# Second layer of a fused transformer: the attention product and the transposed key scores move from between two substitutions into the second one, and each inverse is fetched three quarters through the substitution before it

## Chip, cores and metric

One core of one Trainium2 chip. The time is the device time of one execution in microseconds (us); each figure for a kernel is the median of several runs.

## What is computed

Four batches of 256 tokens with 256 channels pass through two layers. Each layer gates the input with a bidirectional recurrence, adds an attention block, gates again and adds a feed-forward block (ternary weights in layer 0; eight experts, two per token, in layer 1). The change touches only layer 1's attention, cut here to what matters (16 heads of 16, per batch):

```python
s = einsum('bihd,bjhd->bhij', k, k) * scale          # rotated keys with themselves
p = softmax over j < i of s                           # strictly lower triangle
A = eye(T) + p * beta                                 # unit lower triangular, 256 x 256 per head
u = solve_triangular(A, v, lower=True)                # forward substitution
attn = softmax over j <= i of (q k^T * scale)
o = einsum('bhij,bjhd->bihd', attn, u) @ Wo
```

## The kernel before, in words

Every engine runs its own in-order stream. All streams are generated from one list of steps, `ORDER`, written by `make_order`; VectorE alone follows `DVE_ORDER`, which `lag` derives from it by holding a side step back until the next half of the chain has been issued. A step is a tuple (kind, ..., batch, index), and each engine does its own part of it at that place of its list: for `("solve", b, s, half)` TensorE multiplies, VectorE copies the result out of PSUM, and SyncE (SP) issues four small DMAs that move the solution to where the attention product reads it.

The triangular solve of a batch is a chain of eight block rows. `solve b s` multiplies the inverse of a 32x32 diagonal block with the right side (PE line 886, copied by VectorE line 1842); `update b s` multiplies the result with the blocks below (PE line 1117), and VectorE turns it (line 1828) and forms the next right side (line 1831). Each of the two steps is done in two halves of eight heads. The chain needs, per batch:

- `kscores` in five groups (k with k, strictly causal): TensorE, then VectorE maxima (lines 1660 to 1669), then ScalarE exponentials with row sums (line 1385). `kmax` turns the maxima (PE line 1013, ScalarE copy line 1344, four DMAs), `kdiag` recomputes the diagonal blocks transposed (TensorE, ScalarE line 1363), `den` and `blocks` prepare them on VectorE (lines 1800 to 1811), and GpSimd (POOL) inverts them (from line 2052 to 2061). `inverse` is VectorE's transposition of that inverse into place (line 1820); POOL's next `blocks` waits for it, since it works in one buffer.
- `kprobs` in four groups: the transposed k by k scores (TensorE, ScalarE line 1370). They are the factors that `update` reads.

Beside it runs the causal attention: `scores` in eight groups (TensorE; maxima on VectorE, lines 1679 and 1680), `minus` and `max` (VectorE lines 1687 to 1693, PE line 1013, ScalarE line 1344, one DMA), `probs` in eight groups (TensorE, ScalarE lines 1354 and 1355), `pv` (attention times solution: 64 matmuls of TensorE, ScalarE copy line 1397), `otr`, `oT`, `wo` (PE lines 1060, 1070, 886) and the next `gate`.

`pv b` waits until all DMAs of the solution of batch b have landed (semaphore `u_moved`), and VectorE waits for the same before it copies the first link of batch b + 1, because that overwrites their source. `kscores`, `kprobs`, `kdiag`, `scores`, `probs`, `pv`, `otr`, `oT` and `wo` share a ring of two PSUM slots ("mid"): each waits on TensorE until the slot of the step two before it was given back by the engine that reads it.

The lists `ahead[b]` in `make_order` hold the side work of batch b; `spread` deals it out evenly behind the 15 units of the chain (`solve 0`, then `update` and `solve` in turn). Before, the loop put `inverse b` in front of `solve b 0`, and behind the chain of batch b three groups of `kprobs b + 2`, `pv b`, and the fourth group.

## Time and profile before

| | us |
|---|---|
| median of 3 runs (793.16 to 796.17) | 794.1 |
| the profiled execution's own time | 791.78 |
| its span, first to last instruction | 789.9 |
| PE busy / DVE busy / ACT busy / POOL busy | 515.3 / 555.2 / 326.1 / 213.7 |
| mean granted TensorE clock (share of full speed) | 0.776 |
| layer 1's four substitutions, in the trace | about 428.9 to 628.6 |

The page gives busy time by engine, the span in 40 slices, the DMA queues, the chain that ended last and the costliest groups. Behind it stand views of the trace: tables by stretch, the timeline of an engine (start, duration, engine, line, operation, and in brackets the idle time before it with the engine or queue that ended it), the chain in order of time, and groups by line. A timeline row can hold several instructions that follow each other closely (x32); its duration runs from the first start to the last end, and can reach into the next step.

### The profile page before, as it was taken

How to read it: one execution, taken by the hardware profiler on the slowest of the kernel's cores; microseconds unless marked ns; L12 is line 12 of the kernel's file. 1: busy time of each engine (PE TensorE's matmuls, PEld its weight loads, DVE VectorE, ACT ScalarE, POOL GpSimd, SP SyncE). 2: the span in 40 equal slices, each digit the busy share in tenths (PEclk: the TensorE clock that was granted, in tenths of full speed). 3: DMA queues.
4: the chain of work that ended last, by engine and by line, in shares of the span. 5: the costliest groups of instructions: out<-in, count | busy, mean ns of one | idle time of the engine just before them, and what ended most of it. 6: DMA issues, size and time to landing. Idle time of an engine off the chain costs nothing. (4 is left out here: it accounts for less than half of the span.)

```text
span 789.9 us, 18230 instructions
## 1 busy us (share of the span) xinstructions
PE 515.3 (65%) x7549; PEld 424.6 (54%) x7549; DVE 555.2 (70%) x1116; ACT 326.1 (41%) x755; POOL 213.7 (27%) x313
## 2 busy tenths in 40 slices
PE   0362655885696770446557467677877874799995
PEld 0251544774575560334445355456665653699995
DVE  6999699797859966685673677456466536668861
ACT  4344343543456422016444600451321334367771
POOL 2000000000000000100884870881683001335443
PEclk9876856896698985675567575768798956699999
DMA  8145023050000010463016033002102148257622
GB/s 312 38 95 121 1 62 59 1 116 6 1 2 1 21 34 0 101 151 74 4 40 127 5 78 57 6 7 49 61 10 62 13 160 280 80 148 200 202 27 27
DMA packets 48211, 56.07 MB, mean 71 GB/s; under 512 B 25136, under 2 KB 42048, under 8 KB 43648
## 3 DMA queue, kind: packets, MB, share of 16 engines
q1 hardware_dynamic: 44784, 49.90, 24.3%
q0 software_dynamic: 3344, 4.99, 3.3%
q8 instruction: 60, 0.98, 0.5%
q14 instruction: 23, 0.19, 0.1%
HBM read 43.15 MB, written 10.49 MB: 68 GB/s over the span
## 5 line engine op out<-in xcount | busy, mean ns | idle before, releaser
L886 PE MATMUL psum<-arena 32*32 32x16 f32 (+22 forms) x5713 | 357.0, 272 | 213.5 <-DVE arena L1608 76.2
L886 PEld LDWEIGHTS psum<-arena 128*32 128x32 f32 (+8 forms) x5713 | 283.5, 127 | 285.9 <-DVE arena L1608 79.8
L2061 POOL TENSOR_TENSOR arena<-arena 128x31 f32<-128x31 f32 (+15 forms) x124 | 68.3, 551 | 9.7
L2059 POOL TENSOR_TENSOR arena<-arena 128x31 f32<-128x31 f32 (+15 forms) x124 | 64.6, 521 | 9.7
L1385 ACT ACTIVATE psum<-psum,arena 128x256 f32<-128x256 f32 (+7 forms) x128 | 45.7, 363 | 30.4 <-DVE arena L1669 30.1
L1679 DVE TENSOR_REDUCE arena<-psum 128x2 f32<-128x512 f32 (+1 forms) x48 | 41.3, 861 | 13.4 <-PE psum L886 12.8
L1578 DVE TENSOR_TENSOR_SCAN arena<-arena 128x255 f32<-128x255 f32 x64 | 42.5, 726 | 11.4 <-ACT arena L1297 11.3
L1354 ACT ACTIVATE arena<-psum 128x512 f32<-128x512 f32 (+1 forms) x48 | 35.4, 737 | 36.1 <-PE psum L886 36.0
L2040 POOL DMA_DIRECT2D arena<-wq x1 | 0.9, 862 | 171.8 <-PE psum L886 171.8
L1297 ACT ACTIVATE arena<-arena 128x255 f32<-128x255 f32 x64 | 27.2, 498 | 46.4 <-DVE arena L1564 46.4
L2085 POOL DMA_INDIRECT out<-arena x16 | 31.2, 1947 | 48.6 <-DVE arena L1985 46.5
L2075 POOL DMA_INDIRECT arena<-dispatched,arena x16 | 19.7, 1229 | 87.0 <-DVE arena L1952 83.3
L1967 DVE TENSOR_TENSOR fc_second_parts<-arena,fc_first_parts 128x2048 fp32r<-128x2048 f32 x16 | 36.6, 2289 | 7.8 <-ACT fc_first_parts L1489 7.7
L886 PE MATMUL psum<-input_first_parts,fc_first_parts 128*128 128x256 f32 x128 | 38.9, 304 | 1.3 <-DVE input_second_parts L1961 1.3
L1564 DVE TENSOR_TENSOR_SCAN arena<-arena 128x256 f32<-128x256 f32 x64 | 39.0, 671 | 0.5
L1461 ACT ACTIVATE psum<-psum,arena 128x256 f32<-128x256 f32 x64 | 24.6, 448 | 35.5 <-PE psum L886 35.5
L1117 PE MATMUL psum<-arena 32*32 32x224 f32 (+6 forms) x896 | 37.3, 311 | 1.7 <-issue 1.5
L886 PE MATMUL psum<-fc_first_parts,hidden_first_parts 128*128 128x256 f32 x128 | 36.8, 288 | 2.5 <-DVE hidden_second_parts L1978 2.5
L886 PE MATMUL psum<-input_second_parts,fc_first_parts 128*128 128x256 f32 x128 | 38.0, 297 | 0.0
L886 PE MATMUL psum<-input_first_parts,fc_second_parts 128*128 128x256 f32 x128 | 37.9, 296 | 0.0
L1828 DVE STREAM_TRANSPOSE arena<-psum 128x64 f32<-128x64 f32 x56 | 13.8, 246 | 33.8 <-PE psum L1117 33.0
L886 PE MATMUL psum<-fc_second_parts,hidden_first_parts 128*128 128x256 f32 x128 | 36.2, 283 | 0.0
(186 smaller groups left out, 936.3 us busy)
## 6 DMA issues: line engine op xcount, KB each, us to landing
arena<-fc SPq DMA_DIRECT2D x16, 1024.0 KB, 5.0
arena<-parts SPq DMA_DIRECT2D x40, 256.0 KB, 4.6
parts<-arena SPq DMA_DIRECT2D x16, 384.0 KB, 3.5
arena<-parts SPq DMA_DIRECT2D x40, 128.0 KB, 5.2
arena<-arena SPq DMA_DIRECT2D x128, 8.0 KB, 1.8
arena<-xT SPq DMA_DIRECT2D x1, 1024.0 KB, 10.1
arena<-w1T SPq DMA_DIRECT2D x1, 1024.0 KB, 10.1
arena<-w2T SPq DMA_DIRECT2D x1, 1024.0 KB, 12.1
```

The source lines that it names most:

```text
L886: return nc.tensor.matmul(out, lhsT, rhs, start=start, stop=stop)
L1117: last = nc.tensor.matmul(acc(half)[rows, qq, (s + 1) * BLK:T], ublk[rows, s, q, :], later[b % 2][s][rows, q, :], start=s == 0 and qq == 0 ...
L1297: A(scan[s + 1][:, ct, 0:T - 1], scan[s][:, ct, 0:T - 1], ACT.Copy, scale=back[:, i:i + 1]).then_inc(scaled, 1)
L1354: step_(A(prob[:, hs, 0:T], hi, ACT.Exp, scale=scale))
L1385: ins = A(s_, s_, ACT.Exp, bias=nbias[:, n:n + 1], accum_out=ncc[b][:, n:n + 1])
L1564: ins = V.tensor_tensor_scan(scan[s][:, ct, :], dd, src[:, ct, bt(b)], 0.0, ALU.mult, ALU.add)
L1578: st(V.tensor_tensor_scan(scan[s][:, ct, T - 2::-1], dd, scan[s + 1][:, ct, T - 2::-1], scan[s][:, ct, T - 1:T], ALU.mult, ALU.add))
L1679: st(V.tensor_reduce(mneg[:, H + j * n:H + (j + 1) * n], hi, axis=AX.X, op=ALU.max, negate=True))
L1967: V.tensor_tensor(second[:], fcw[e % NW][i], first[:].bitcast(F32), ALU.subtract).then_inc(w_second[i], 1)
L2059: link(G_.tensor_tensor(tmp, A3[:, k + 1:BLK, k:k + 1].to_broadcast([P, rows, w]), X3[:, k:k + 1, 0:w].to_broadcast([P, rows, w]), ALU.mult))
L2061: ins = G_.tensor_tensor(X3[:, k + 1:BLK, 0:w], X3[:, k + 1:BLK, 0:w], tmp, ALU.add)
L2085: G_.indirect_dma_start(out=d["out"], out_offset=bass.IndirectOffsetOnAxis(ap=ids[:, 2 * e + s:2 * e + s + 1], axis=0), in_=eo[e % 2][:, s ...
```

## The change

For b = 0, 1, 2 it places the side work anew. `pv b`, the first entry of the old list of batch b + 1, and all four groups of `kprobs b + 2` (where there is such a batch) become the first entries of `ahead[b + 1]`, so that they are dealt out behind the links of the substitution of batch b + 1. `inverse b + 1` becomes an entry of `ahead[b]` at three quarters of its length. `inverse 0` stands in front of the loop, and `solve 0` of a batch stands alone as first unit. Behind the last batch `route`, `count` and `pv 3` are where they were. `lag` recognises the start of a substitution by `solve` in place of `inverse`. No instruction is added or removed.

```diff
     for b in range(B):
-
-        solve = [[("inverse", b), ("solve", b, 0, 0), ("solve", b, 0, 1)]]
+        if b + 1 < B:
+            ahead[b + 1] = [[("pv", 1, b)]] + ahead[b + 1][:1] + ([[step] for step in groups("kprobs", 1, b + 2)] if b + 2 < B else []) \
+                + ahead[b + 1][1:]
+            ahead[b].insert(len(ahead[b]) * 3 // 4, [("inverse", b + 1)])
+    o += [("inverse", 0)]
+    for b in range(B):
+
+        solve = [[("solve", b, 0, 0), ("solve", b, 0, 1)]]
         for s in range(1, NS):
             solve += [[(kind, b, s - (kind == "update"), half) for half in range(2)] for kind in ("update", "solve")]
         o += sum(spread(solve, ahead[b]), [])
-        if b + 2 < B:
-            o += groups("kprobs", 1, b + 2)[:3]
-        else:
-            o += [("route", i) for i in range(B - 1) if b == B - 1] + [("count",)] * (b == B - 1)
-        o += [("pv", 1, b)]
-        if b + 2 < B:
-            o += groups("kprobs", 1, b + 2)[3:]
+    o += [("route", i) for i in range(B - 1)] + [("count",), ("pv", 1, B - 1)]
...
-        if step[0] == "inverse":
+        if step[0] == "solve":
             solving = True
```

Three places show what moves. The first is ScalarE behind batch 0's substitution: line 1344 is the copy of `max`, 1370 `kprobs 2`, 1397 `pv 0`, 1385 `kscores 3`. Before, and then now:

```order
L1344 ACTIVATE arena<-psum 64x128
L1370 ACTIVATE arena<-psum 128x896
L1370 ACTIVATE arena<-psum 128x768
L1370 ACTIVATE arena<-psum 128x128
L1370 ACTIVATE arena<-psum 128x640
L1370 ACTIVATE arena<-psum 128x256
L1397 ACTIVATE arena<-psum 128x1024
L1370 ACTIVATE arena<-psum 128x512
L1370 ACTIVATE arena<-psum 128x384
L1385 ACTIVATE psum,arena<-psum,arena 128x256 x4
```

```order
L1344 ACTIVATE arena<-psum 64x128
L1397 ACTIVATE arena<-psum 128x1024
L1385 ACTIVATE psum,arena<-psum,arena 128x256 x4
L1370 ACTIVATE arena<-psum 128x896
L1370 ACTIVATE arena<-psum 128x768
L1370 ACTIVATE arena<-psum 128x128
L1370 ACTIVATE arena<-psum 128x640
L1370 ACTIVATE arena<-psum 128x256
L1370 ACTIVATE arena<-psum 128x512
L1370 ACTIVATE arena<-psum 128x384
L1385 ACTIVATE psum,arena<-psum,arena 128x32 x4
```

The product now comes first, and all of `kprobs 2` stands between the first group of `kscores 3` and the other four. On TensorE, `solve 1 0` now stands in front of `pv 0`, and `update 1 0` behind `pv 0` and the first group of `kscores 3`, with two groups of `kprobs 2` on either side of `solve 1 1`.

The second is TensorE in batch 1: line 1013 is `kmax 3`, 1060 `otr 0`, 32x16 x16 a `solve`, the rows of 32x32 and 32x512 are `kdiag 3`, those of 128x256 and 128x128 the first `probs 1`, and line 1117 is `update` (32x160 is `update 1 2`). Before, and then now:

```order
L1013 MATMUL psum<-arena 64x128
L1060 MATMUL psum<-arena 128x128 x8
L886 MATMUL psum<-arena 32x16 x16
L886 MATMUL psum<-arena 32x32 x64
L886 MATMUL psum<-arena 32x512 x4
L886 MATMUL psum<-arena 32x32 x64
L886 MATMUL psum<-arena 32x512 x4
L886 MATMUL psum<-arena 128x256
L886 MATMUL psum<-arena 128x128
L886 MATMUL psum<-arena 128x256
L886 MATMUL psum<-arena 128x128 x5
L1117 MATMUL psum<-arena 32x160 x16
```

```order
L1013 MATMUL psum<-arena 64x128
L1117 MATMUL psum<-arena 32x160 x16
L1060 MATMUL psum<-arena 128x128 x8
L886 MATMUL psum<-arena 32x32 x64
L886 MATMUL psum<-arena 32x512 x4
L886 MATMUL psum<-arena 32x32 x64
L886 MATMUL psum<-arena 32x512 x4
L886 MATMUL psum<-arena 32x16 x16
L886 MATMUL psum<-arena 128x256
L886 MATMUL psum<-arena 128x128
L886 MATMUL psum<-arena 128x256
L886 MATMUL psum<-arena 128x128 x5
```

`update 1 2` now stands in front of `otr 0` and `kdiag 3`, and `solve 1 3` directly behind `kdiag 3`; on VectorE the copy of `solve 1 3` comes behind `blocks 3`, which before stood in front of `update 1 2`.

The third is VectorE in the end of batch 2: pairs of lines 1679 and 1680 are `scores 3`, 1842 copies of `solve`, 1828 and 1831 `update`, 1687 to 1693 `minus 3`, 1820 `inverse 3`. Before, the end of the batch and the start of the next; then now, around `solve 2 5`:

```order
L1842 COPY arena<-psum 128x2x16 x2
L1679 TENSOR_REDUCE arena<-psum 128x2
L1680 TENSOR_REDUCE arena<-psum 128x2
L1679 TENSOR_REDUCE arena<-psum 128x2
L1680 TENSOR_REDUCE arena<-psum 128x2
L1687 TENSOR_SCALAR arena<-arena 128x32
L1692 CAST arena<-arena 128x2x16
L1693 TENSOR_TENSOR arena<-arena 128x2x16
L1820 STREAM_TRANSPOSE arena<-arena 128x32x32
L1842 COPY arena<-psum 128x2x16 x2
```

```order
L1842 COPY arena<-psum 128x2x16 x2
L1679 TENSOR_REDUCE arena<-psum 128x2
L1680 TENSOR_REDUCE arena<-psum 128x2
L1820 STREAM_TRANSPOSE arena<-arena 128x32x32
L1828 STREAM_TRANSPOSE arena<-psum 128x64
L1831 SCALAR_TENSOR_TENSOR arena<-arena 128x16 x2
L1828 STREAM_TRANSPOSE arena<-psum 128x64
L1831 SCALAR_TENSOR_TENSOR arena<-arena 128x16 x2
L1679 TENSOR_REDUCE arena<-psum 128x2
L1680 TENSOR_REDUCE arena<-psum 128x2
```

`inverse 3` left the place behind `minus` and stands behind `solve 2 5`, in front of VectorE's part of `update 2 5`; one of eight `scores` is in front of it and seven are behind it. `inverse 1` and `inverse 2` stand likewise behind `update 0 5` and `update 1 5`, with four and eight `scores` behind them.

## Rows read from the trace of the kernel before

**Rows 1.** The page, busy time of the engines, share of the span, instructions.

```profile
PE 515.3 (65%) x7549; PEld 424.6 (54%) x7549; DVE 555.2 (70%) x1116; ACT 326.1 (41%) x755; POOL 213.7 (27%) x313
```

**Rows 2.** Timelines of PE and DVE around the end of batch 0's substitution.

```profile
455.21 5.78 PE L886 MATMUL psum<-arena 128*128 128x256 f32 x160 [1.51 <-DVE arena L1608]
...
484.36 0.41 DVE L1842 COPY arena<-psum 128x32 f32<-128x32 f32 x2 [0.78 <-PE psum L886]
...
491.41 0.31 PE L1013 MATMUL psum<-arena 128*64 128x128 bf16 x1 [1.79 <-DVE arena L1693]
...
500.99 1.72 PE L1117 MATMUL psum<-arena 32*32 32x224 f32 x32
```

**Rows 3.** The chain in order of time: start, us, engine and line.

```profile
494.58 4.57 PE psum L886 x64
...
512.24 2.92 ACT psum L1385 x16
```

**Rows 4.** Timeline of PE where an attention product waits for the solution's DMAs.

```profile
598.26 0.32 PE L1013 MATMUL psum<-arena 128*64 128x128 bf16 x1 [2.13 <-DVE arena L1693]
599.42 5.34 PE L886 MATMUL psum<-arena 128*32 128x256 f32 x96 [0.85 <-issue]
...
632.49 5.37 PE L886 MATMUL psum<-arena 128*32 128x256 f32 x64 [1.11 <-DMA arena<-arena]
```

**Rows 5.** Groups of ACT by line, 552 to 566 us: busy, mean ns, idle before.

```profile
L1370 ACT ACTIVATE arena<-psum 128x896 f32<-128x896 f32 (+6 forms) x7 | 3.7, 598 | 0.8 <-PE psum L886 0.8
```

**Rows 6.** Timelines of ACT, PE and DVE in batch 1's substitution.

```profile
505.86 0.45 ACT L1385 ACTIVATE psum<-psum,arena 128x256 f32<-128x256 f32 x1 [4.79 <-DVE arena L1669]
...
519.62 0.27 ACT L1344 ACTIVATE arena<-psum 64x128 bf16<-64x128 bf16 x1
...
523.72 3.26 PE L886 MATMUL psum<-arena 98*32 98x32 bf16 x144 [3.38 <-DMA arena<-arena]
...
525.83 1.02 ACT L1363 ACTIVATE arena<-psum 128x1024 f32<-128x1024 f32 x1 [5.95 <-PE psum L886]
...
527.12 1.92 DVE L1811 STREAM_TRANSPOSE arena<-arena 128x1024 f32<-128x1024 f32 x1
...
532.15 1.08 PE L1117 MATMUL psum<-arena 32*32 32x128 f32 x32
...
543.08 0.38 DVE L1831 SCALAR_TENSOR_TENSOR arena<-arena 128x16 f32<-128x16 f32 x2
```

**Rows 7.** Timelines of POOL and DVE: POOL's last inversion, and the inverse's transposition.

```profile
557.50 1.91 POOL L2052 TENSOR_TENSOR arena<-arena 128x1024 f32<-128x1024 f32 x1 [21.43 <-DVE arena L1820]
...
599.57 1.97 DVE L1820 STREAM_TRANSPOSE arena<-arena 128x1024 f32<-128x1024 f32 x1 [1.37 <-POOL arena L2061]
```

**Rows 8.** DVE in the end of batch 2: timeline, then groups, 584 to 599 us.

```profile
588.60 0.25 DVE L1828 STREAM_TRANSPOSE arena<-psum 128x64 f32<-128x64 f32 x1
...
L1679 DVE TENSOR_REDUCE arena<-psum 128x2 f32<-128x512 f32 x8 | 5.4, 679 | 0.0
L1680 DVE TENSOR_REDUCE arena<-psum 128x2 f32<-128x256 f32 x8 | 3.3, 411 | 0.0
```

**Rows 9.** Timeline of PE: the first two updates of batch 3.

```profile
605.01 1.72 PE L1117 MATMUL psum<-arena 32*32 32x224 f32 x32 [0.24 <-DVE arena L1842]
...
608.73 1.50 PE L1117 MATMUL psum<-arena 32*32 32x192 f32 x32
```

**Rows 10.** Timeline of POOL: the same operation twice in batch 0's inversion.

```profile
392.25 0.63 POOL L2061 TENSOR_TENSOR arena<-arena 128x231 f32<-128x231 f32 x1
...
407.00 0.96 POOL L2061 TENSOR_TENSOR arena<-arena 128x231 f32<-128x231 f32 x1
```

**Rows 11.** Table by stretch: us, busy (x instructions) of PE, PEld, DVE, ACT, POOL, clock, DMA, GB/s.

```profile
494.60:498.00 3.40, 3.40 (x41) 2.27 (x45) 0.00 (x0) 0.98 (x2) 3.11 (x4) 0.50 0.00 0
498.00:500.00 2.00, 1.87 (x92) 1.61 (x84) 0.13 (x2) 0.83 (x1) 1.61 (x6) 0.99 0.03 8
...
500.00:552.60 52.60, 35.83 (x982) 26.59 (x983) 33.37 (x101) 22.27 (x87) 31.39 (x58) 0.77 0.14 23
```

## The prediction

> **What bounds the kernel now.** The page first: no engine is busy throughout, VectorE (DVE) 70%, TensorE (PE) 65% [rows 1]. So the span is made of waits between in-order engines, and the change, which only moves steps, must be judged where they hand over. I read the timelines of PE, DVE, ACT and POOL from 428 to 650 us, at four places.
>
> Between batches 0 and 1, PE runs `max 1` at 491.41 and the first update of batch 1 at 500.99 [rows 2]: 9.6 us, nearly all PE's own work, of which `pv 0` is 4.57 [rows 3]. DVE has little to do there, so `inverse 1` lies beside it for nothing. In the first half of batch 1, ACT and PE wait in turn for the groups of `kscores 3`: from the first exponential at 505.86 to the copy of `kmax` at 519.62 are 13.8 us, PE then waits 3.38 us for the DMAs of `kmax`, and `update 1 3` starts at 532.15 [rows 6]. In the end of each batch DVE is the pace: the last two updates, six `scores` and `minus` of batch 2 take from 588.60 to `max 3` at 598.26 [rows 4, 8], and a pair of maxima costs 0.68 and 0.41, about 1.0 us together. Last, POOL: from the start of the last inversion (557.50) to `inverse 3` (599.57) are 42.1 us, and DVE already waits 1.37 us for it [rows 7]. `inverse 2` to `inverse 3` is 1.97 + 0.15 + 42.1 = 44.2 us, which no order of the other engines shortens.
>
> **The change, term by term.** In batch 0 `inverse 1` (1.97 us) enters DVE's list among the `scores`; the wait of 0.78 in front of `solve 0 6` [rows 2] and a like one take some 1.2 of it, so +0.7. `gate 3` comes one update earlier on DVE; PE waits 1.51 us for it in front of the projection [rows 2], and I take half, -0.7. Together 0 (bounds -1.5 and +2.0).
>
> *First hand-over.* `solve 1 0` stands in front of `pv 0`, but DVE may not copy it, nor PE start `pv 0`, until the last DMAs of batch 0 have landed. The price is seen in front of `pv 2`, which starts 1.2 us after `max 3` without `kprobs` in between [rows 4]; the label there is "issue", but the last `pv`, in the same position, waits on the DMAs by name [rows 4]. So `pv 0` starts at 492.6, ends at 497.2, and the first group of `kscores 3` with its hops (half of the 1.84 us that lay between `pv 0` and the update before) lets `update 1 0` start at 498.1: **-2.9**. Only `kprobs` left this place; `pv 0` still stands in front of the first update on an in-order engine. This bounds the gain of the title's move.
>
> *Batch 1 up to `inverse 2`.* The first exponentials come 4.87 us behind the update [rows 2, 6], at 503.0, and take 1.9. ACT then does the seven exponentials of `kprobs 2`, 3.7 us [rows 5], to 508.6. PE's `kprobs` wait for the two slots that ACT frees, `update 1 1` follows at about 508 and DVE's part of it ends near 510. Only then are the other four groups of `kscores 3` begun: DVE some 2.4 us each (half of those 4.87, an estimate), ACT 2.9 us for a group of eight exponentials [rows 3]. Group 1 is exponentiated from 512.6 and group 2 to 518.4; group 3 waits for a slot and for `solve 1 2`, 520.0 to 522.9; group 4 (half) to 524.3, the copy of `kmax` to 524.5, before 519.9: **4.6 late**. `kdiag 3` keeps its distance of 3.8 us: 528.3. Its 2.1 us on PE (523.72 to 525.83), 1.02 on ACT and some 2.1 of `blocks` on DVE, 1.92 of it line 1811 [rows 6], now stand in front of DVE's copy of `solve 1 3`, at 533.5, while `update 1 2` has got past them. So `update 1 3` starts at about 533.7, against 532.15: +1.5. Behind it two `probs` and `oT` more are left than before and one `scores` less, which I put at 0.5 after its cover by PE's waits (an estimate). `update 1 5`, whose last row ended at 543.46 [rows 6], ends at 545.5: **+2.0** against before, so batch 1 has lost 4.9. Bounds: -2.9 if `kprobs` cost nothing there, and +4.9 if the later update does not win back what `kmax` lost.
>
> *Inversion.* `inverse 2` runs 545.5 to 547.5, POOL needs 0.15 + 42.1, `inverse 3` runs 589.7 to 591.7. Before it ended at 601.54: **-9.9**. By its own chain DVE gets there at about the same time (`update 2 5` was at 588.60 before [rows 8]): `kprobs 3` in front of batch 2's links then costs little, because POOL sets the time.
>
> Row first: the same POOL operation took 0.63 us and, at 407.00, 0.96 us [rows 10]. The Trainium skill, SBUF — State Buffer, section "Who interferes with whom", says that a VectorE instruction with two SBUF inputs and a GpSimd instruction that reads SBUF exclude each other for a whole instruction. This speaks against putting more chain work of DVE under an inversion: were ten more operations held for 0.33 us each, `inverse 3` would come 3.3 us later and the sum would be +8.2 in place of +4.9. The traced inversion already lies beside DVE's chain, so the sum goes by 42.1.
>
> *From `inverse 3` to batch 3.* DVE now has behind it what took 588.60 to 598.26, 9.66 us, and one more `scores`, 1.0, with 0.8 for slots: 11.5, where before it was free at once. `max 3` falls at 603.2, the DMA wait and the copy add 1.5, `update 3 0` starts at 604.7; before 605.01 [rows 9]: **-0.3**. All 9.9 us are given back, because the inverse was moved from beside PE's work into the stretch that DVE bounds.
>
> *Batch 3.* `pv 2`, 4.9 us [rows 4], has left the place in front of `update 3 0` and stands between it and `solve 3 1`. The two updates were 3.7 apart [rows 9], with `otr 2` and `solve 3 1` behind the first; now `pv 2` is added to them, 8.6: **+4.9**. DVE's part of `otr 2` then holds `solve 3 2`: +0.3 after cover.
>
> Sum: -0.3 + 4.9 + 0.3 = +4.9 us against the profiled execution's own 791.78, so 796.7. The median of the runs is 794.1, 2.3 above that execution, so the forecast is **799.0**, 0.6% slower. About 0.5%, 4 us, is what a measurement can tell from no change.
>
> **Rivals.** *Batch 1 hides the four groups.* For it: PE is busy for only 35.8 of 52.6 us there [rows 11] and waits 3.38 in one piece. Against it: the waits are for ACT and DMAs, in the phase in which ACT gets 3.7 us more. If only 1.0 of the 4.9 is left, `inverse 2` comes 3.9 earlier and POOL's chain hands it on in full: +1.0, 795.1, no change that can be told.
>
> *Faster: PE at its upper clock from `pv 0` to `inverse 2`.* Mechanism and place: `pv 0` began after a halting stretch of PE and ran at a granted 0.50 (1.2 GHz), 41 matmuls in 3.4 us, then at 0.99 (2.4 GHz) 92 instructions in 1.87 [rows 11]; batch 1 ran at 0.77. If side work between the links keeps PE busier, `pv 0` takes 2.9 us in place of 4.57 (its 3.4 us at 0.50 halved), `update 1 1`, `kdiag 3` and their like perhaps 3 less, `pv 2` 2 less (estimates from the same ratio), and with the first rival's 3.9 that is 4.9 - 10.6 = -5.7: 788.4. It decides when `update 1 5` ends before about 538, 5 us earlier than in the trace of before. Against it: the waits of the scores and of the DMAs stay in front of both products, and the `kscores` phase gets more waits.
>
> *Slower still.* If `kmax`'s delay is not won back, `update 1 5` is at +4.9 and the sum +7.8: 801.9. With POOL held up as well it is a few us more.
>
> That the change does not do what it says is excluded by the listed order.
>
> **How the numbers follow.** Forecast 0.50 (its own range 796.5 to 804.5, the further delay within it), first rival 0.36, faster 0.14. The range 788.5 to 804.5 reaches down to the faster rival's time, and up to the further delay with 2.6 for a longer inversion. Faster by over 0.5%: 0.14; within: 0.36; slower: 0.50.
>
> **What would show it.** Right: `max 1` to the first update of batch 1 in about 6.7 us with a DMA wait in front of `pv 0`; `kmax 3` copied 20 us or more after the first exponential of `kscores 3`; `inverse 2` about 10 us earlier, and 44 us from it to `inverse 3`, DVE waiting there a little or not at all; `inverse 3` to `update 3 0` some 13 us; 8 to 9 us between the first two updates of batch 3. Wrong: `update 1 5` over earlier than at 541, PE at full clock through `pv 0` or `pv 2`, or an inversion well off 42 us.

## The result, and the profile after

The changed kernel takes 804.7 us (median of 4 runs, 801.4 to 808.4) against 794.2 for the kernel before beside it: a ratio of 1.0131, 95% interval 1.0082 to 1.018. It is slower by 1.3%, some 10 us. The prediction was 799.0 (+4.9), range 788.5 to 804.5: the sign was right, the size half of what came, the time just outside the range. A second measurement of the same kernel (`after_again` below) gave 803.0 us against 793.5, a ratio of 1.013.

The profiled execution of the changed kernel took 808.41 us, the slowest of the four; a second profile, that of `after_again`, took 798.89, the fastest of six. So both are read, and only what they agree on is taken for the change's. First the page of the changed kernel, to set beside [rows 1]. The counts of instructions are the same, but PE is busy for 12.5 us more (5.4 in the second profile), at a mean granted clock of 0.760 (0.766 in the second) against 0.776 before. So a part of the loss lies in PE's clock and the rest in waits; no run here separates the two as a whole.

```profile
PE 527.8 (65%) x7549; PEld 433.5 (54%) x7549; DVE 556.2 (69%) x1116; ACT 325.2 (40%) x755; POOL 212.7 (26%) x313
```

The timelines give the loss by stage. Every number in this table is the distance in us between the starts of two PE rows, `update b s` being the row of line 1117 with 224 - 32 s columns; the first stage starts at DVE's row of `inverse 0` (426.89, 430.50, 427.50, 429.94 and 430.26 us in the five profiles). Up to there no step was moved, and from `update 3 6` to the end of the span the five agree within 1 us. The last two columns are experiments told below.

| stage | before | after | after again | kp_late | kp2_only |
|---|---|---|---|---|---|
| inverse 0 to update 1 0 | 74.1 | 71.7 | 69.9 | 71.9 | 70.5 |
| update 1 0 to 1 3 | 31.2 | 38.4 | 37.3 | 28.9 | 27.9 |
| update 1 3 to 1 6 | 15.9 | 18.1 | 18.1 | 18.7 | 16.2 |
| update 1 6 to 2 0 | 17.8 | 15.0 | 15.0 | 15.6 | 17.8 |
| update 2 0 to 2 2 | 8.6 | 11.4 | 11.1 | 11.3 | 8.5 |
| update 2 2 to 2 5 | 13.7 | 15.2 | 13.9 | 14.1 | 13.7 |
| update 2 5 to 2 6 | 4.5 | 7.0 | 7.0 | 7.0 | 4.6 |
| update 2 6 to 3 0 | 12.4 | 9.0 | 9.0 | 9.0 | 12.2 |
| update 3 0 to 3 1 | 3.7 | 8.9 | 8.0 | 8.1 | 3.7 |
| update 3 1 to 3 6 | 15.9 | 16.0 | 16.0 | 16.0 | 15.9 |
| all | 197.7 | 210.5 | 205.0 | 200.4 | 190.9 |

The three hand-overs are indeed shorter, by about 3 us each. All of that and more is lost inside the batches: 6 to 7 us in front of `update 1 3`, 2 to 3 each where `inverse 2`, then `pv 1` with `kprobs 3`, and then `inverse 3` now stand, 4 to 5 behind `update 3 0`.

The largest loss, in the timeline of PE after the change; the matching rows of before are [rows 2, 6]:

```profile
495.57 0.31 PE L1013 MATMUL psum<-arena 128*64 128x128 bf16 x1 [1.86 <-DVE arena L1693]
...
502.20 1.72 PE L1117 MATMUL psum<-arena 32*32 32x224 f32 x32
503.85 0.57 PE L886 MATMUL psum<-arena 98*32 98x224 bf16 x16
509.04 3.11 PE L886 MATMUL psum<-arena 98*32 98x192 bf16 x128 [4.63 <-ACT psum L1385]
512.08 2.78 PE L1117 MATMUL psum<-arena 32*32 32x192 f32 x32
...
521.60 1.81 PE L886 MATMUL psum<-arena 96*32 96x96 bf16 x96 [5.18 <-ACT psum L1385]
...
527.70 0.32 PE L1013 MATMUL psum<-arena 128*64 128x128 bf16 x1 [2.59 <-DVEq L1672]
527.95 2.36 PE L1117 MATMUL psum<-arena 32*32 32x160 f32 x32
...
534.47 2.31 PE L886 MATMUL psum<-arena 98*32 98x32 bf16 x161 [2.31 <-DMA arena<-arena]
538.14 2.54 PE L886 MATMUL psum<-arena 32*32 32x16 f32 x23 [1.35 <-issue]
540.61 1.84 PE L1117 MATMUL psum<-arena 32*32 32x128 f32 x32
```

And ACT in the same stretch: first group of `kscores 3`, `kprobs 2` (line 1370), second group, copy of `kmax 3` (line 1344).

```profile
507.06 0.45 ACT L1385 ACTIVATE psum<-psum,arena 128x256 f32<-128x256 f32 x1 [4.19 <-DVE arena L1669]
...
508.87 0.93 ACT L1370 ACTIVATE arena<-psum 128x896 f32<-128x896 f32 x1
...
518.65 0.26 ACT L1385 ACTIVATE psum<-psum,arena 128x32 f32<-128x32 f32 x1 [5.34 <-DVE arena L1669]
...
530.30 0.29 ACT L1344 ACTIVATE arena<-psum 64x128 bf16<-64x128 bf16 x1
```

The rows of 96x... are `kscores`, those of 98x224 to 98x192 `kprobs 2`. After the first group ACT does `kprobs 2`, and 11.6 us lie between the first exponential of group 0 (507.06) and that of group 1 (518.65). The copy of `kmax` comes 28.1 us behind `update 1 0`, before 18.6 [rows 2, 6]. Behind it come the wait for the DMAs (2.31, before 3.38), `kdiag` and `blocks`; they now stand in front of the copy of `solve 1 3`, where before they stood in front of `update 1 2` and of DVE's part of it. From the copy of `kmax` to `update 1 3` it is 10.3 us in both profiles and 12.5 before, so `update 1 3` is late because the copy of `kmax` is.

The second profile shows the same waits on PE; its copy of `kmax`, from ACT, stands last:

```profile
497.37 1.72 PE L1117 MATMUL psum<-arena 32*32 32x224 f32 x32
...
504.48 3.10 PE L886 MATMUL psum<-arena 98*32 98x192 bf16 x128 [4.90 <-ACT psum L1385]
...
515.85 1.82 PE L886 MATMUL psum<-arena 96*32 96x96 bf16 x96 [4.63 <-ACT psum L1385]
...
521.94 0.32 PE L1013 MATMUL psum<-arena 128*64 128x128 bf16 x1 [2.58 <-DVEq L1672]
...
528.45 2.31 PE L886 MATMUL psum<-arena 98*32 98x32 bf16 x161 [2.16 <-DMA arena<-arena]
...
534.63 1.83 PE L1117 MATMUL psum<-arena 32*32 32x128 f32 x32
```

```profile
524.34 0.29 ACT L1344 ACTIVATE arena<-psum 64x128 bf16<-64x128 bf16 x1
```

Next POOL's last inversion, and behind it DVE's `inverse 3`, in the first profile after the change, beside [rows 7]:

```profile
555.43 1.90 POOL L2052 TENSOR_TENSOR arena<-arena 128x1024 f32<-128x1024 f32 x1 [24.10 <-DVE arena L1820]
...
596.73 0.25 POOL L2061 TENSOR_TENSOR arena<-arena 128x31 f32<-128x31 f32 x1
```

```profile
600.66 1.90 DVE L1820 STREAM_TRANSPOSE arena<-arena 128x1024 f32<-128x1024 f32 x1
```

POOL is done at 596.98; DVE comes to `inverse 3` 3.7 us later, without waiting (1.7 later in the second profile). POOL does not set this time, DVE's chain does; what made that chain late in batch 2, the experiment on the transfer shows. Last, `max 3`, `update 3 0`, `pv 2`, `otr 2` and `update 3 1` on PE:

```profile
614.63 0.32 PE L1013 MATMUL psum<-arena 128*64 128x128 bf16 x1 [1.79 <-DVE arena L1693]
...
616.09 3.21 PE L1117 MATMUL psum<-arena 32*32 32x224 f32 x32 [0.28 <-DVE arena L1842]
619.23 3.96 PE L886 MATMUL psum<-arena 128*32 128x256 f32 x96
623.96 1.09 PE L1060 MATMUL psum<-arena 128*128 128x128 f32 x8 [0.77 <-ACT arena L1397]
624.98 1.50 PE L1117 MATMUL psum<-arena 32*32 32x192 f32 x32
```

`update 3 0` follows `max 3` by 1.5 us, and `update 3 1` follows it by 8.9 where it was 3.7 [rows 9]: the product only changed places with the update.

### The profile page after: what moved, and what is told of

Its sections match the earlier page's. It is cut to its first block and busy times, and to the rows that moved or that the text cites. A ratio compares the mean times of both kernels' runs of the same rounds, so it can differ in the third digit from the quotient of the medians.

```text
span 806.5 us, 18234 instructions
## 1 busy us (share of the span) xinstructions
PE 527.8 (65%) x7549; PEld 433.5 (54%) x7549; DVE 556.2 (69%) x1116; ACT 325.2 (40%) x755; POOL 212.7 (26%) x313
## 5 line engine op out<-in xcount | busy, mean ns | idle before, releaser
L886 PE MATMUL psum<-arena 32*32 32x16 f32 (+20 forms) x5713 | 364.0, 272 | 212.7 <-DVE arena L1608 75.8
L886 PEld LDWEIGHTS psum<-arena 128*32 128x32 f32 (+8 forms) x5713 | 289.2, 128 | 287.7 <-DVE arena L1608 79.1
L1385 ACT ACTIVATE psum<-psum,arena 128x256 f32<-128x256 f32 (+7 forms) x128 | 45.7, 370 | 36.3 <-DVE arena L1669 35.5
L1679 DVE TENSOR_REDUCE arena<-psum 128x2 f32<-128x512 f32 (+1 forms) x48 | 41.4, 863 | 14.1 <-PE psum L886 13.3
L1578 DVE TENSOR_TENSOR_SCAN arena<-arena 128x255 f32<-128x255 f32 x64 | 42.5, 727 | 11.4 <-ACT arena L1297 11.3
L2085 POOL DMA_INDIRECT out<-arena x16 | 31.2, 1948 | 48.9 <-DVE arena L1985 47.1
L1117 PE MATMUL psum<-arena 32*32 32x224 f32 (+6 forms) x896 | 41.5, 337 | 3.2 <-DVE arena L1842 3.2
## 6 DMA issues: line engine op xcount, KB each, us to landing
arena<-w1T SPq DMA_DIRECT2D x1, 1024.0 KB, 10.5
```

Source lines behind the costliest of these rows:

```text
L886: return nc.tensor.matmul(out, lhsT, rhs, start=start, stop=stop)
L1117: last = nc.tensor.matmul(acc(half)[rows, qq, (s + 1) * BLK:T], ublk[rows, s, q, :], later[b % 2][s][rows, q, :], start=s == 0 and qq == 0 ...
L1385: ins = A(s_, s_, ACT.Exp, bias=nbias[:, n:n + 1], accum_out=ncc[b][:, n:n + 1])
L1578: st(V.tensor_tensor_scan(scan[s][:, ct, T - 2::-1], dd, scan[s + 1][:, ct, T - 2::-1], scan[s][:, ct, T - 1:T], ALU.mult, ALU.add))
L1679: st(V.tensor_reduce(mneg[:, H + j * n:H + (j + 1) * n], hi, axis=AX.X, op=ALU.max, negate=True))
L2085: G_.indirect_dma_start(out=d["out"], out_offset=bass.IndirectOffsetOnAxis(ap=ids[:, 2 * e + s:2 * e + s + 1], axis=0), in_=eo[e % 2][:, s ...
```

## The experiments

Theories, as they are called in the expectations. **K**: the place of `kprobs` among `kscores` and `kmax` is the loss. **I**, later **V**: the inverse costs its 1.97 us because it lies where VectorE is the pace; **B**: it costs that at any place in the chain. **P**: `pv` only changes places. **L**: the 1 MB transfer of expert weights, which SyncE now issues behind its wait for `pv 1`, halts TensorE. **S**: the longer lists shift all other steps between the links. **W**: `kprobs` cost their own work wherever they stand. Each ratio is to the kernel before in the same set of runs, with its 95% interval; the changed kernel is 1.0131 and, again, 1.013.

**One part back, or one part alone.** Three kernels undo one part; `inv_only` and `pv_only` do one alone. The lines that differ from the changed kernel:

```diff
 inv_back
-            ahead[b].insert(len(ahead[b]) * 3 // 4, [("inverse", b + 1)])
-        solve = [[("solve", b, 0, 0), ("solve", b, 0, 1)]]
+        solve = [[("inverse", b), ("solve", b, 0, 0), ("solve", b, 0, 1)]]
 pv_back: in the entries of ahead[b + 1], and behind the links of every batch
-[[("pv", 1, b)]] +
+        o += [("pv", 1, b)]
 kp_back: likewise; the fourth group follows pv, which has left
-([[step] for step in groups("kprobs", 1, b + 2)] if b + 2 < B else []) +
+            o += groups("kprobs", 1, b + 2)[:3]
+            o += groups("kprobs", 1, b + 2)[3:]
 inv_only: pv_back and kp_back together
 pv_only: inv_back and kp_back together
```

> Everything of the change except the place of the inverse: inverses 1 to 3 stand again in front of the first link of their batch, the products and the keys' products stay behind it. Theory I (the inverse in the score stretch, which VectorE paces, costs about 2 us in each of three batches, and its place beside TensorE's work was free): 3 to 6 us faster than the changed kernel's 804.7, so 799 to 802. Theory K (the products of kprobs between the first links delay the copy of kmax and then the links): 804 to 807, since the inverse then comes no earlier and POOL's 42 us count again in batch 2. Theory P (the product pv only lies in front of the second link in place of the first, no gain): no difference from this part, 804.

> The product pv of batches 0 to 2 stands again in front of the first update of the next batch, inverse and kprobs stay moved. Theory P: what the first links lose is won back between first and second update, so within 1.5 us of the changed kernel, 803 to 806, and the transfer of 1 MB of expert weights in batch 2 is issued early again. Theory L (the late transfer and the halts of TensorE in batch 2 cost several us): 799 to 801.

> The kprobs of two batches on stand again at the boundary (three groups, pv is behind the first link, so the fourth follows them), inverse and pv stay moved. Theory K: batch 1 loses the 5 us or so that the copy of kmax came late, and batch 2 what kprobs 3 costs there, while the hand-over in front of update 1 0 is again about 9.6 instead of 6.6 us in batches 0 and 1: 4 to 6 us faster than the changed kernel, 799 to 801. Theory I: kprobs cost about the same in either place, 803 to 806.

> The kernel before with the inverse alone moved to three quarters of the batch ahead. Theory I: 3 to 6 us slower than the kernel before, 797 to 800. Theory K: the inverse's 2 us per batch are covered or won back since inverse 3 no longer waits for POOL's 42 us behind a late inverse 2: within 2 us of before, 792 to 796.

> The kernel before with pv alone moved behind the first link; kprobs stay at the boundary and the inverse in front of the first link. Theory P (pv only lies in front of the second link in place of the first): within 0.2% of before, u 3 0 earlier by 4 to 5 us and u 3 1 not. Theory L: slower by 0.3% or more, since the transfer of 1 MB in batch 2 falls behind pv here too.

| run | ratio to before | interval |
|---|---|---|
| inv_back | 1.0121 | 1.0083 to 1.0158 |
| pv_back | 1.0101 | 1.0067 to 1.0135 |
| kp_back | 1.0061 | 1.0037 to 1.0085 |
| inv_only | 1.0068 | 1.0037 to 1.0099 |
| pv_only | 1.0058 | 1.0039 to 1.0078 |

`kprobs` back gives 0.7% back, with an interval that does not touch that of the second measurement of the change: K. With the inverse back, the links that it left are 2.3 and 2.7 us shorter in the trace (`update 2 5` to `2 6` takes 4.7), but the time gains 0.1%, which is nothing, so theory I, which wanted 3 to 6 us, falls in that form. Yet the inverse alone costs 0.7%, and `pv` alone 0.6% where P wanted nothing; L's 0.3% or more came, but L is not thereby shown. The parts do not add: `pv` and inverse together (`kp_back`) cost 0.6%, no more than either alone. Two things in the trace of `pv_only` go some way to tell why. `update 1 0` to `1 3` takes 34.9 us there and 31.7 in `kp_back`, whose list is one entry longer, so that `otr` and the rest fall between other links. And with `pv` gone from the boundary and `inverse 3` still there, DVE waits for POOL:

```profile
606.61 1.90 DVE L1824 STREAM_TRANSPOSE arena<-arena 128x1024 f32<-128x1024 f32 x1 [2.03 <-POOL arena L2065]
```

This is `inverse 3`, 43.9 us behind `inverse 2`, and `update 3 0` follows 2.7 us after this start; in `kp_back`, without the inverse there, `update 2 6` to `3 0` is 7.0 us instead of 10.2. `pv_back`, 0.3% below the change, lies between P and L and decides nothing.

**The inverse, and what the insertion shifts.** `inv_joined` is `inv_only` with TensorE's order left as it was before, row for row; `all_joined` does the same to the whole change; `inv_link4` puts the inverse at another place in every batch.

```diff
 inv_joined, all_joined
-            ahead[b].insert(len(ahead[b]) * 3 // 4, [("inverse", b + 1)])
+            ahead[b][len(ahead[b]) * 3 // 4 - 1] += [("inverse", b + 1)]
 all_joined
+            ahead[b + 1][0] = [("pv", 1, b)] + ahead[b + 1][0] + (groups("kprobs", 1, b + 2) if b + 2 < B else [])
 inv_link4, pv_link4, all_link4 (from inv_only, from kp_back, from the changed kernel)
-        o += sum(spread(solve, ahead[b]), [])
+        links = sum(spread(solve, ahead[b]), [])
+        if b + 1 < B:
+            links.insert(links.index(("solve", b, 4, 1)) + 1, ("inverse", b + 1))
+        o += links
 pv_link4, too
+            ahead[b + 1][0] = [("pv", 1, b)] + ahead[b + 1][0]
```

> The kernel before with the inverse alone moved, but joined to the step at three quarters instead of inserted as an entry of its own, so that TensorE's order stays that of the kernel before, row for row, and only VectorE's inverses 1 to 3 move. (The insertion alone cost 0.7%.) Theory V (VectorE's own 1.97 us in the stretch that it paces is what costs): as slow as the insertion, 0.4 to 0.7% above before. Theory S (the insertion makes the list longer and so shifts other steps between the links, after which TensorE halts more and its clock falls in batch 2): within 0.2% of before, and TensorE's granted clock near 1.00 up to the fifth update of batch 2.

> The whole change, but pv and kprobs are joined to the first entry of the next list, and the inverse to the one at three quarters, so that the other steps are spread over the links as in the kernel before: all of pv and kprobs lie between the first and the second link. Theory S: the kscores groups are reached after the same number of links as before, and much of the loss goes: ratio 1.002 to 1.007. Theory K: the same products in the same kscores phase, the ratio stays at 1.010 to 1.014.

> The kernel before with the inverse of the next batch alone moved, behind solve b 4, where VectorE waits for TensorE in each batch, with TensorE's order that of the kernel before. Theory V (an inverse costs its 1.97 us only where VectorE is the pace): within 0.3% of before, against 0.7 to 0.9% for three quarters. Theory B (the boundary loses nothing when the inverse leaves it, and any place in the chain costs about 2 us): 0.6 to 0.9% slower.

> As the last, and pv moved behind the first link too, joined to the first step there, so that the other steps are spread as before; kprobs at the boundary. Theory V: the boundary in front of batches 1 to 3 gets shorter by 2 to 4 us each, and the first pair of links takes most of it back; 0.2% faster to 0.3% slower than before. Theory B: 0.5 to 0.9% slower.

> The changed kernel with the inverse behind solve b 4 in place of three quarters. Theory V: 4 to 6 us faster than the changed kernel, ratio 1.006 to 1.009. Theory B: no difference, 1.012 to 1.014.

| run | ratio to before | interval |
|---|---|---|
| inv_joined | 1.0085 | 1.0052 to 1.0119 |
| all_joined | 1.0179 | 1.0153 to 1.0205 |
| inv_link4 | 1.0051 | 1.0021 to 1.0082 |
| pv_link4 | 1.0076 | 1.005 to 1.0102 |
| all_link4 | 1.0089 | 1.0061 to 1.0116 |

S falls for the inverse: with TensorE's order unchanged the inverse alone still costs 0.85%, and the joined change is the slowest of all. (In `all_joined` all four `kprobs 2` stand in front of `update 1 0`, which starts at 80.3 behind `inverse 0` instead of 74.1; K, too, had not foreseen more than 1.4%.) Why the boundary gives nothing back for an inverse that leaves it, the tables by stretch show. From `update 2 6` to `update 3 0`, before, then in `inv_joined`, then in `inv_link4`, the columns as in [rows 11]:

```profile
592.60:605.00 12.40, 8.18 (x179) 5.64 (x177) 7.65 (x22) 0.78 (x2) 5.84 (x15) 0.72 0.33 94
```

```profile
599.20:611.80 12.60, 9.58 (x182) 6.71 (x185) 5.11 (x19) 0.78 (x2) 0.00 (x0) 0.54 0.32 91
```

```profile
598.00:610.40 12.40, 8.11 (x179) 5.59 (x177) 5.50 (x21) 0.72 (x2) 0.00 (x0) 0.72 0.32 94
```

DVE has 2.5 and 2.2 us less to do, and the stretch is no shorter. In `inv_link4` PE is busy as long as before (8.1 us) at the same granted clock (0.72), so the inverse lay beside PE's work there and set nothing. In `inv_joined` the same steps of PE took 9.6 us at a granted 0.54; by `inv_link4` that is not why nothing was gained. In the links the inverses of `inv_joined` cost 0.9, 1.6 and 2.3 us (`update b 5` to `b 6`); its hand-over to batch 1 (`update 0 6` to `update 1 0`) is 2.1 longer than before, but that of `inv_link4` is not (15.25 us against 15.35). So the inverses cost in the links and save nothing at the boundary, as long as `pv` stands there beside them.

Whether their place in the links matters is not settled: `solve b 4` costs 0.5%, three quarters 0.7 and 0.85%, with overlapping intervals. The interval of `inv_link4` holds V's 0.3% at its lower end and most of B's 0.6 to 0.9% at its upper. `pv_link4` agrees with B and not with V. `all_link4` lies below the change by 0.4%, in V's range and under B's, but its interval overlaps with the change's.

**The transfer.** In `load_early` SyncE issues the weights in front of its wait for `pv`:

```diff
+                    if b >= 2 and s == 0:
+                        wait_pe(sp, ("probs", 1, b - 1, NGS[1] - 1))
+                        for e, i in (((1, 1),), ((0, 0),))[b - 2]:
+                            load_half(e, i)
                     if b and s == 0:
                         wait_pe(sp, ("pv", 1, b - 1))
...
-                    for e, i in (((1, 1),), ((0, 0),), ((0, 1), (1, 0)))[b - 1]:
+                    for e, i in (((0, 1), (1, 0)) if b == B - 1 else ()):
```

> The changed kernel, with the transfers of expert weights that stand in front of pv 1 and pv 2 issued by SyncE before its wait for pv, at solve 2 0 and solve 3 0, as early as in the kernel before. Theory L (the late transfer halts TensorE for 1.8 us in batch 2, and the clock falls behind it): 2 to 3 us faster than the changed kernel, ratio to before 1.009 to 1.011, no halt of 1.8 us in front of update 2 2. Theory K (the products between the links cost by themselves): the ratio stays at 1.012 to 1.014.

Measured: 1.0107 (1.0083 to 1.0132), as L expected, but inside the interval of the changed kernel, whose second measurement is 1.013. In the time it is not settled. The traces show more. TensorE's order is the same in both kernels; these are PE's rows from `solve 2 2` up to `update 2 2`, with the first `probs 2` between them, in the changed kernel and then in `load_early` (line numbers four higher; there the `probs` follow so closely that they share the row of `solve 2 2`):

```profile
581.00 0.99 PE L886 MATMUL psum<-arena 32*32 32x16 f32 x24 [0.24 <-DVE arena L1831]
583.84 1.25 PE L886 MATMUL psum<-arena 98*128 98x256 bf16 x8 [1.84 <-issue]
```

```profile
577.69 1.56 PE L890 MATMUL psum<-arena 32*32 32x16 f32 x32 [0.29 <-DVE arena L1835]
579.18 1.29 PE L1121 MATMUL psum<-arena 32*32 32x160 f32 x32
```

In the changed kernel PE halts for 1.84 us (1.55 in the second profile) in front of `probs 2`; in `load_early` the halt is gone. From `update 2 0` to `update 2 2` the 16 DMA engines are busy for 0.37 of the time in the first and 0.10 in the other, and the stage takes 11.4 and 11.1 us with the late transfer, 9.0 with the early one, 8.6 before. Two kernels below repeat the pair: 11.4 us in `late_link4`, 8.7 in `late_l4_load`. So this part of L is right, and `pv 1` and `kprobs 3` themselves add little there. How the transfer holds PE is not shown: the row says "issue", which names no releaser, and in `pv_only` and `kp_back`, where the transfer comes as late but these `probs` come 4.5 instead of 10.2 us behind `update 2 0`, the stage is 9.1 us. A part of the gain is lost again because POOL then sets the time of `inverse 3`, 44.0 us behind `inverse 2` in `load_early`:

```profile
594.04 1.91 DVE L1824 STREAM_TRANSPOSE arena<-arena 128x1024 f32<-128x1024 f32 x1 [0.52 <-POOL arena L2065]
```

**Where `kprobs` stand.** `kp_late` leaves all as changed and puts the four `kprobs 2` behind `kmax`:

```diff
+            after_kmax = next((i + 1 for i, g in enumerate(ahead[b + 1]) if g[0][0] == "kmax"), 1)
-            ahead[b + 1] = [[("pv", 1, b)]] + ahead[b + 1][:1] + ([[step] for step in groups("kprobs", 1, b + 2)] if b + 2 < B else []) \
-                + ahead[b + 1][1:]
+            ahead[b + 1] = [[("pv", 1, b)]] + ahead[b + 1][:after_kmax] \
+                + ([[step] for step in groups("kprobs", 1, b + 2)] if b + 2 < B else []) + ahead[b + 1][after_kmax:]
```

What stands behind which link (S) and update (U) of batch 1, then:

```
before   S0: kscores0 | U0: kscores1 kscores2 | S1: kscores3 kscores4 | U1: kmax otr | S2: kdiag den blocks
after    S0: pv kscores0 | U0: kprobs0 kprobs1 | S1: kprobs2 kprobs3 | U1: kscores1 kscores2 kscores3 | S2: kscores4 kmax | U2: otr kdiag den blocks
kp_late  S0: pv kscores0 | U0: kscores1 kscores2 | S1: kscores3 kscores4 | U1: kmax kprobs0 kprobs1 | S2: kprobs2 kprobs3 | U2: otr kdiag den blocks
```

> The changed kernel with the four kprobs of batch 2 behind the copy of kmax in place of ahead of the four kscores groups of batch 1; all else, kprobs 3 in batch 2 too, as in the changed kernel. Theory K (kmax is copied right in front of kdiag, and the DMAs of kmax, blocks and the copy of solve 1 3 queue behind it): the products then lie in the wait for these DMAs, update 1 3 comes 4 us earlier or more, ratio 1.005 to 1.009. Theory W (the kprobs cost their own work wherever they stand between the links): 1.011 to 1.014.

Measured: 0.9999 (0.9974 to 1.0024). The whole loss is gone, more than K expected, by the place of four steps, which lets `kscores` and `kmax` come earlier. (Its profiled execution, 797.48 us, is the slowest of its twelve, so its sum in the table is on the high side.) PE and then ACT in its trace (line numbers are one higher):

```profile
501.88 1.72 PE L1118 MATMUL psum<-arena 32*32 32x224 f32 x32
...
508.76 1.81 PE L887 MATMUL psum<-arena 96*32 96x64 bf16 x96 [4.34 <-ACT psum L1386]
...
519.65 0.32 PE L1014 MATMUL psum<-arena 128*64 128x128 bf16 x1
519.89 2.44 PE L887 MATMUL psum<-arena 98*32 98x224 bf16 x112
...
525.38 1.95 PE L887 MATMUL psum<-arena 98*32 98x32 bf16 x161
...
530.73 1.93 PE L1118 MATMUL psum<-arena 32*32 32x128 f32 x32
```

```profile
520.59 0.27 ACT L1345 ACTIVATE arena<-psum 64x128 bf16<-64x128 bf16 x1
520.79 3.54 ACT L1371 ACTIVATE arena<-psum 128x896 f32<-128x896 f32 x7
```

`kmax` is copied 18.7 us behind `update 1 0`, as before. PE does `kprobs 2` (519.89) while the DMAs of `kmax` run, and `kdiag` (525.38) has no wait for them any more, where it was 3.38 before [rows 6] and 2.31 after. So W falls: in the one place `kprobs 2` cost 6 to 7 us, in the other they fill a wait. From `update 1 0` to `update 1 3` that is 2.3 us less than in the kernel before (28.9 against 31.2) and 8.4 to 9.6 less than in the changed kernel. Some 3 of the latter lie in PE's clock: for the same work PE is busy for 17.8 us at a granted 0.76 in `kp_late`, for 21.4 and 20.6 us at 0.67 and 0.70 in the two profiles of the changed kernel. The rest are waits.

**What is left then.** From `kp_late`: the inverse behind `solve b 4`, then the early transfer as well, then `kprobs 3` behind the first `scores` of batch 2 as well; and the changed kernel once more.

```diff
 late_link4: kp_late with the links.insert of all_link4; late_l4_load: with the transfer of load_early
 late_l4_load_k3: in place of after_kmax
+        if b + 2 < B:
+            at = next(i for i, g in enumerate(ahead[b + 1]) if g[0][0] == ("kmax" if b == 0 else "scores")) + 1
+            ahead[b + 1] = ahead[b + 1][:at] + [[step] for step in groups("kprobs", 1, b + 2)] + ahead[b + 1][at:]
```

> The changed kernel once more, unaltered, to have its time and a second profile beside the others. All theories: ratio to before 1.010 to 1.015; in batch 1 the copy of kmax again some 7 us later than before.

> kprobs 2 behind the copy of kmax, and the inverse behind solve b 4 in place of three quarters. Theory V (an inverse costs its 1.97 us only where VectorE is the pace): 2 to 4 us faster than kprobs 2 behind kmax alone, ratio to before 0.995 to 0.998, and update 2 5 to update 2 6 back from 7.0 to about 4.6 us. If it is 0.999 to 1.002, the place in the chain does not matter.

> As late_link4, and SyncE issues the expert weights in front of its wait for pv 1 and pv 2, as early as in the kernel before. Theory L: another 1 to 2 us, ratio 0.993 to 0.996. Otherwise as late_link4, within 0.15%.

> As late_l4_load, and the four kprobs 3 stand behind the first scores of batch 2, where ScalarE has nothing to do, in place of behind its first step. Theory K: update 2 0 to update 2 2 gets 2 to 3 us shorter and the scores lose less than 1 of it, ratio 0.990 to 0.994. If kprobs 3 cost their own work wherever they stand between the links, as late_l4_load.

| run | ratio to before | interval |
|---|---|---|
| after_again | 1.013 | 1.0095 to 1.0164 |
| late_link4 | 1.0031 | 0.9997 to 1.0065 |
| late_l4_load | 1.0008 | 0.9974 to 1.0042 |
| late_l4_load_k3 | 1.001 | 0.9986 to 1.0035 |

The change repeats; its copy of `kmax` was 4.1 us late by the distance to `inverse 0` (the expectation said 7), 8.3 by the distance to `update 1 0`. The other three are all as fast as the kernel before, and their intervals overlap with that of `kp_late`: none of the three theories is borne out in the time. In the traces two of the stages did shorten: `update 2 5` to `2 6` takes 4.4 us in `late_link4`, as V expected, and `update 2 0` to `2 2` takes 8.7 in `late_l4_load`, as L expected. One row of `late_l4_load` is worth having:

```profile
579.96 1.92 DVE L1827 STREAM_TRANSPOSE arena<-arena 128x1024 f32<-128x1024 f32 x1 [2.14 <-POOL arena L2068]
```

This is `inverse 3`, 44.0 us behind `inverse 2`, and here DVE does wait for POOL, as in `load_early`: the bound of 44.2 us that the prediction used exists, but in the changed kernel DVE comes later than that.

**One part that pays.** The last pair leaves `pv` and the inverses where they were before, and moves `kprobs` alone, behind `kmax`: 2, or 2 and 3 (the latter behind the first `scores`).

```diff
 kp2_only, from the kernel before
+            if b + 2 < B and b == 0:
+                at = next(i for i, g in enumerate(ahead[b + 1]) if g[0][0] == ("kmax" if b == 0 else "scores")) + 1
+                ahead[b + 1] = ahead[b + 1][:at] + [[step] for step in groups("kprobs", 1, b + 2)] + ahead[b + 1][at:]
...
+        late = groups("kprobs", 1, b + 2) if b == 1 else []
+        o += late[:3] + [("pv", 1, b)] + late[3:]
 kp2_kp3
-            if b + 2 < B and b == 0:
+            if b + 2 < B:
-        o += late[:3] + [("pv", 1, b)] + late[3:]
+        o += [("pv", 1, b)]
```

> The kernel before with the four kprobs 2 alone moved, behind the copy of kmax of batch 1, where TensorE waited 3.4 us for its DMAs; pv, kprobs 3 and the inverses stay at the boundaries. Theory K (order among kscores, kmax and kprobs decides): the hand-over to batch 1 is 2 to 3 us shorter and batch 1 no longer than before: 2 to 5 us faster than before, ratio 0.993 to 0.998. If the hand-over is set by the inverse or by pv, no difference, 0.999 to 1.002.

> As kp2_only, and kprobs 3 behind the first scores of batch 2 in place of the boundary. Theory K: the second hand-over gets 2 to 3 us shorter, and POOL, which needs 44 us from inverse 2 to inverse 3, takes part of that: ratio 0.990 to 0.997. If they cost their work in the links, as kp2_only or slower.

`kp2_only` takes 787.7 us, 0.9917 of the kernel before (0.9891 to 0.9942), and beats both kernels; that is 6.3 us, and the distance from `inverse 0` to `update 3 6` is 6.8 us shorter in its trace. `kp2_kp3` is at 0.9963 (0.9939 to 0.9987): moving `kprobs 3` as well takes half of it back, against K, though the two intervals just touch; why, is not shown (its profile fell on one of its slowest executions, 796.85 us against a median of 790.8). PE and then ACT in `kp2_only`, from `max 1` to `update 1 3` (line numbers two higher):

```profile
493.11 0.32 PE L1015 MATMUL psum<-arena 128*64 128x128 bf16 x1 [1.78 <-DVE arena L1695]
494.20 6.63 PE L888 MATMUL psum<-arena 128*32 128x256 f32 x192 [0.78 <-issue]
500.75 1.72 PE L1119 MATMUL psum<-arena 32*32 32x224 f32 x32
...
514.93 0.31 PE L1015 MATMUL psum<-arena 128*64 128x128 bf16 x1 [2.75 <-DVEq L1674]
...
517.89 2.33 PE L888 MATMUL psum<-arena 98*32 98x224 bf16 x112
...
523.26 2.02 PE L888 MATMUL psum<-arena 98*32 98x32 bf16 x161
...
528.60 1.93 PE L1119 MATMUL psum<-arena 32*32 32x128 f32 x32 [0.31 <-DVE arena L1844]
```

```profile
517.38 0.30 ACT L1346 ACTIVATE arena<-psum 64x128 bf16<-64x128 bf16 x1
```

The hand-over is 7.6 us instead of 9.6, `kdiag` again has no wait for DMAs, and all later stages are as in the kernel before. The four products left a boundary that PE sets (1.9 us) and fill a wait that nothing filled (`update 1 0` to `1 3` is 3.3 us shorter). The other 1.7 of the 6.8 us lie between `inverse 0` and `max 1`, where no step was moved, so they are not the move's. Nor are the 3.3 the filled wait alone: the longer list also puts the second group of `kscores 3` in front of `update 1 0`, so `kmax` is copied 16.6 us behind it instead of 18.6, and puts `update 1 2` in front of `kdiag`. No run separates these.

## Why the prediction was half right

The prediction's own terms, against the two profiles after the change. First where each came out later than forecast (us; minus is earlier):

| from, to | forecast | first profile | second profile |
|---|---|---|---|
| inverse 0 to update 1 0 | 71.2 | +0.5 | -1.3 |
| update 1 0 to update 1 3 | 35.6 | +2.8 | +1.7 |
| update 1 3 to inverse 2 | 11.8 | +1.0 | +1.0 |
| inverse 2 to inverse 3 | 44.2 | +3.1 | +1.5 |
| inverse 3 to update 3 0 | 15.0 | +0.4 | +0.4 |
| update 3 0 to update 3 1 | 8.6 | +0.3 | -0.6 |

- **First hand-over, -2.9.** Right in kind and about in size: `max 1` to `update 1 0` takes 6.6 us in the first profile (495.57 to 502.20) and 5.6 in the second (491.76 to 497.37), forecast 6.7.
- **"4.6 late", then "`update 1 3` starts at about 533.7".** The mechanism was right: ACT does `kprobs 2` between two groups of `kscores`, `kmax` is late, and `kdiag` and `blocks` get in front of `solve 1 3`. The size was not: from `update 1 0` to the copy of `kmax` the forecast was 26.4 us, and it measured 28.1 and 27.0. The 0.5 us for what stands behind `update 1 3` was also too little, by 1.0. So `inverse 2` came later than forecast by 4.3 and 1.3 us.
- **"`kprobs 3` in front of batch 2's links then costs little, because POOL sets the time".** This is the step that failed in kind. POOL did not set the time: it had ended 3.7 and 1.7 us before DVE came to `inverse 3`, and from `inverse 2` to `inverse 3` it was 47.3 and 45.7 us, not 44.2. `kprobs 3` itself cost little there. What the walk put at nothing is the 1 MB transfer that moves behind `pv 1`: with it PE halts for 1.84 and 1.55 us and `update 2 0` to `update 2 2` takes 11.4 and 11.1 us; with the transfer issued early it takes 9.0, and the 44.0 us of POOL come back, DVE waiting 0.52 us for it (`load_early`).
- **"All 9.9 us are given back".** Right: from the start of `inverse 3` to `update 3 0` it is 15.4 us in both profiles, against 5.4 before, 10.0 more.
- **`pv 2` between `update 3 0` and `solve 3 1`, +4.9.** Right: +5.2 and +4.3.
- **A price from the skill.** By the Trainium skill, SBUF — State Buffer, section "Who interferes with whom", a VectorE instruction with two SBUF inputs and a GpSimd instruction that reads SBUF exclude each other. The prediction priced this at 3.3 us if more of DVE's chain came under the inversion, and did not follow it. The two profiles do not show it: POOL took 41.6 and 42.0 us in the two profiles and 42.0 before, but DVE was busy for only 19.8 and 21.5 us beside it, against 22.7 before, so the condition did not arise.
- **Rivals.** That batch 1 hides the four groups is refuted by both profiles, and so is PE at its upper clock: from `max 1` to `update 1 0` the granted clock was 0.57 and 0.70 in the two, and 0.67 and 0.70 from there to `update 1 3`, where the upper level (2.4 GHz) is 1.00. The further delay (801.9) was nearest; its +4.9 at `update 1 5` measured +6.4 and +3.4.

The stages sum to +12.8 us in the first profile and +7.3 in the second, the medians to +9.5 to +10.5. The forecast of +4.9 lacked 2.7 to 3.8 us in batch 1 and 1.5 to 3.1 in batch 2; that a second measurement lies inside the range does not make these two steps right. The experiments add what the walk could not: the loss hangs on where four products stand. Behind `kmax` they fill a wait, and the changed kernel is as fast as the one before.

## What to carry to other kernels

Before side work is moved between the links of a chain, look at what it is put in front of: work that ends in a DMA on which the chain depends (here `kscores` up to `kmax`) must not be delayed, and the wait for that DMA is where side work is free. Ask also what else hangs on a moved step: here a transfer of 1 MB went with `pv`, and came where it halted PE. Try each part of a combined move alone: here a half of one part, `kprobs 2`, put in the right place, gained 0.8%, and the other two parts together cost 0.6%. An operation that lies beside another engine's work at a hand-over is free there as long as that work stays: at the boundary to batch 3, taking the inverse away shortened nothing.

## What was not expected of the hardware

The same rows can cost twice as much from one kernel to the next, although the order around them is the same. `update 1 2` and the rows with it in `late_l4_load_k3` and in `late_l4_load`, which do not differ up to there, by the tables by stretch:

```profile
526.70:529.00 2.30, 2.30 (x37) 1.37 (x33) 0.63 (x3) 0.98 (x2) 0.00 (x0) 0.50 0.12 11
```

```profile
523.70:525.00 1.30, 1.30 (x45) 0.94 (x33) 0.41 (x3) 1.23 (x4) 0.00 (x0) 1.00 0.15 22
```

The row of `update 1 2` itself took 2.36 us in the one and 1.29 in the other, and the granted clock was 0.50 (1.2 GHz) and 1.00 (2.4 GHz). What set it apart is not shown. And two profiles of the changed kernel itself differ by 9.5 us in time, 3.0 of it ahead of `inverse 0`, where nothing was moved. Most of the stage lengths agree within 1 us in both all the same; a single profile's sum does not.
